# A neighbourhood-attention stage written out over its 28 strips, with another order of work on the engines

## The chip, the cores and the metric

The kernel runs on one core of a Trainium2 chip. The metric is the device time of one execution in microseconds (us), the median of three runs. TensorE (PE in the profile, PEld for its weight loads), VectorE (DVE), ScalarE (ACT), GpSimd (POOL) and SyncE (SP, which here only issues transfers) run side by side and are ordered by semaphores.

## The reference, cut to what matters

Eight images of 128 channels and 56x56 positions go through one block each: group norm, 7x7 neighbourhood attention with 16 heads of 8 channels, a projection and a residual; then full attention over the 3136 positions with 8 heads; then a small dequantised FFN. The part that is changed is the neighbourhood attention:

```python
for a in range(7):
    ka = take(k, si + a, axis=2)                 # si, sj: window start, clipped at the border
    for c in range(7):
        kac = take(ka, sj + c, axis=3)
        logits.append(einsum('bhijd,bhijd->bhij', q, kac) + bias)
attn = softmax(stack(logits, -1), axis=-1)
# out = sum over a, c of attn[..., t] * v at the same neighbour; then out @ proj_w.T + proj_b
```

## The kernel before, in words

All five engines run one loop over the eight images (`b`). Inside an image the stages follow each other: group norm and the q, k, v projections; the neighbourhood stage; projection, layer norm and more projections; the full attention in 14 units (7 blocks of 448 positions, 2 groups of 4 heads); the FFN. The full attention and the other stages are written out; they are not changed.

The neighbourhood stage takes the image in 28 strips of two rows. A strip has 14 units of 2x4 queries, each with a window of 8x10 = 80 keys. All 16 heads and 8 queries of a unit fill the 128 partitions. For strip n:

- POOL `spread_queries` (L467, two instructions): scaled queries times a head mask into `QB`, one of two buffers.
- ACT `keys` (L840): copies the 8 key rows of the window into `KS`, one of two buffers.
- PE `scores` (L602): 112 small float32 matmuls into PSUM banks 0 to 2. These banks exist once, so it waits for the bias additions of the strip before.
- DVE `add_bias` (L1024, five instructions, then L1029): scores plus bias table into the score buffer `SC`, and the negated maximum of each unit.
- POOL `subtract_max` (L472), ACT `exponentials` (L845), DVE `sum_up` (L1033 and L1035: sum and reciprocal), POOL `normalise` (L477): the softmax, in place in `SC`.
- PE `turn` (L613): 14 transposes of `SC` into banks 3, 4, 5, 7; ACT `read_turned` (L853, four instructions) copies them to `PT`.
- PE `values` (L623): 112 small matmuls of the value window `VP` with `PT` into bank 6.
- DVE `finish` (L1040, then L1049 twice): keeps each head's own part and adds it up into `On`.
- SP `load_values` (L374): eight transfers of 70 KB that bring the value window of a strip from DRAM into one of two `VP` buffers, once `values` of the strip two before is done.

`SC` has two buffers, by the strip's parity. Each engine has its order written out by hand, two strips to a pass of an inner loop (`Fori`), with a few strips ahead of and behind the loop outside it. Per strip the orders are:

```
PE    scores(s), turn(s-1), values(s-2)
DVE   add_bias(s), finish(s-2), sum_up(s)
POOL  subtract_max(s), spread_queries(s+2), normalise(s)
ACT   read_turned(s-1), exponentials(s), keys(s+2)
```

An engine takes its instructions in this order, so an instruction that waits holds up all that stand behind it.

Of the kernel before, what the change touches and what calls it, by code (L numbers as in the profile page):

```python
# [15 lines left out]
P = 128  # L16
SIDE = 56
# [112 lines left out]
def hybrid_block(nc, images, x, consts, qkv_wT, rpb, proj_wT, proj_b, Wq, bq, Wk, bk, Wv, bv, Wo, bo,  # L130
# [3 lines left out]
    with ExitStack() as ctx:  # L134
# [54 lines left out]
        KS = part(11088, 2 * WI * WIDE).rearrange("p (s n) -> p s n", s=2)  # L189
        SC = part(15936, 2 * UNITS * KEYS).rearrange("p (s u k) -> p s u k", s=2, u=UNITS)  # L190
# [32 lines left out]
        keys_strip, queries_strip = sem("keys_strip"), sem("queries_strip")  # L223
# [84 lines left out]
        def _(sp):  # L308
# [67 lines left out]
            with sp.Fori(0, images) as b:  # L376
# [10 lines left out]
                load_values(window_row(0), 0)  # L387
                load_values(window_row(1), 1)
                with sp.Fori(1, STRIPS // 2 - 1) as t:
                    for k in range(2):  # L390

                        sp.wait_ge(pv_in, b * STRIPS + (t * 2 + (k - 1 + PRIMED)))
                        apart(sp)
                        load_values(t * 4 + (2 * k - 3), k)
                for k in range(2):
                    s = STRIPS - 2 + k
                    sp.wait_ge(pv_in, b * STRIPS + (s - 1 + PRIMED))
                    load_values(window_row(s), k)
# [44 lines left out]
        def _(pool):  # L443
# [5 lines left out]
            with pool.Fori(0, images) as b:  # L449
# [10 lines left out]
                def spread_queries(tok0, k):  # L460
                    for i in range(QI):
                        src = Qn[:, bass.ds(tok0 + i * SIDE, SIDE)] if not isinstance(tok0, int) else \
                            Qn[:, tok0 + i * SIDE:tok0 + (i + 1) * SIDE]
                        dst = QB[:, k, :, :].rearrange("p u (h i j) -> p u h i j", h=GH, i=QI)[:, :, :, i, :]
                        src = src.rearrange("p (u o j) -> p u o j", o=1, j=QJ).to_broadcast([P, UNITS, GH, QJ])
# [3 lines left out]
                def subtract_max(n, k):  # L469
                    pool.wait_ge(biased, (n + 1) * 6 + PRIMED)  # L470
                    m = NM[:, k, 0:UNITS].rearrange("p (u o) -> p u o", o=1).to_broadcast([P, UNITS, KEYS])
                    nc.gpsimd.tensor_tensor(SC[:, k, :, :], SC[:, k, :, :], m, ALU.add).then_inc(shifted, 1)  # L472

                def normalise(n, k):
                    pool.wait_ge(summed, n * 2 + 2)
                    r = SUMS[:, 1, k, 0:UNITS].rearrange("p (u o) -> p u o", o=1).to_broadcast([P, UNITS, KEYS])
                    nc.gpsimd.tensor_tensor(SC[:, k, :, :], SC[:, k, :, :], r, ALU.mult).then_inc(normalised, 1)  # L477

                wait_freed(pool, b, NQ, NBLK - 1)
                apart(pool)  # L480
                base = b * STRIPS

                def queries(s, k):
                    if not (isinstance(s, int) and s < 2):
                        pool.wait_ge(scores_in, base + (s - 1))
                    spread_queries(s * (QI * SIDE), k)


                queries(0, 0)
                queries(1, 1)  # L490
                with pool.Fori(0, STRIPS // 2 - 1) as t:
                    for k in range(2):
# [3 lines left out]
                for k in range(2):  # L496
                    subtract_max(base + (STRIPS - 2 + k), k)
                    normalise(base + (STRIPS - 2 + k), k)
# [57 lines left out]
        def _(pe):  # L556
# [8 lines left out]
            with pe.Fori(0, images) as b:  # L565
# [26 lines left out]
                def scores(n, k):  # L592
                    pe.wait_ge(keys_strip, n + 1)
                    pe.wait_ge(queries_strip, n * 2 + 2)
                    pe.wait_ge(biased, n * 6 + (PRIMED - 1))
                    apart(pe)
                    win = KS[:, k, :].rearrange("p (y x) -> p y x", x=WIDE)
                    for u in range(UNITS):
                        bk_, at = s_at[u]
                        for g in range(4):  # L600
                            r = slice(32 * g, 32 * g + 32)
                            m = mm(PS[r, bk_, at * KEYS:(at + 1) * KEYS], QB[r, k, u, :],  # L602
                                   win[r, :, u * QJ:u * QJ + WJ], start=True, stop=True,
                                   tile_position=(32 * g, 32 * g))
                    m.then_inc(scores_in, 1)

                def turn(n, k):

                    pe.wait_ge(normalised, n + 1)
                    for c in range(4):  # L610
                        pe.wait_ge(turned_read, n * 4 + (c - 3 + PRIMED))
                        for u in range(4 * c, min(4 * c + 4, UNITS)):
                            m = nc.tensor.transpose(PS[0:KEYS, TURN_BANKS[c], (u % 4) * P:(u % 4 + 1) * P],  # L613
                                                    SC[:, k, u, :], ident)
                        m.then_inc(turned, 1)

                def values(n, k, visit):
                    pe.wait_ge(turned_read, n * 4 + (4 + PRIMED))
                    pe.wait_ge(out_strip, n * 3 + PRIMED)
                    pe.wait_ge(values_in[k], visit)  # L620
# [7 lines left out]
                VIS = 16 * WI  # L628
                per = STRIPS // 2 * VIS

                scores(base, 0)
                scores(base + 1, 1)
                turn(base, 0)
                with pe.Fori(1, STRIPS // 2) as t:
                    scores(base + t * 2, 0)
                    turn(base + (t * 2 - 1), 1)
                    values(base + (t * 2 - 2), 0, b * per + t * VIS)
                    scores(base + (t * 2 + 1), 1)
                    turn(base + t * 2, 0)
                    values(base + (t * 2 - 1), 1, b * per + t * VIS)  # L640
                values(base + (STRIPS - 2), 0, b * per + per)
                turn(base + (STRIPS - 1), 1)
                values(base + (STRIPS - 1), 1, b * per + per)
                pe.wait_ge(out_strip, b * (3 * STRIPS) + 3 * STRIPS + PRIMED)
# [168 lines left out]
        def _(act):  # L813
            nc.scalar.preload_act_table_set("natural_log_exp_and_others")
            act.wait_ge(weights_in, 16 * 22)
            with act.Fori(0, images) as b:
# [15 lines left out]
                wait_freed(act, b, NK, NBLK - 1)  # L832
                act.wait_ge(pads_zero, b * 3 + 3)

                def keys(n, row, k, first):
                    if not first:
                        act.wait_ge(scores_in, n - 1)
                    src = Kn[:, bass.ds(row * WIDE, WI * WIDE)] if not isinstance(row, int) else \
                        Kn[:, row * WIDE:(row + WI) * WIDE]
                    nc.scalar.activation(KS[:, k, :], src, ACT.Copy).then_inc(keys_strip, 1)  # L840

                def exponentials(n, k):
                    act.wait_ge(shifted, n + 1)
                    v = SC[:, k, :, :].rearrange("p u k -> p (u k)")
                    nc.scalar.activation(v, v, ACT.Exp).then_inc(exps, 1)  # L845

                def read_turned(n, k):
                    for c in range(4):
                        act.wait_ge(turned, n * 4 + (c + 1))
                        if c == 0:  # L850
                            act.wait_ge(pv_in, n + (PRIMED - 1))
                        u0, u1 = 4 * c, min(4 * c + 4, UNITS)
                        nc.scalar.activation(PT[0:KEYS, k, u0:u1, :].rearrange("p u e -> p (u e)"),  # L853
                                             PS[0:KEYS, TURN_BANKS[c], 0:(u1 - u0) * P], ACT.Copy).then_inc(turned_read, 1)


                keys(base, window_row(0), 0, True)
                keys(base + 1, window_row(1), 1, True)
                exponentials(base, 0)
                keys(base + 2, window_row(2), 0, False)  # L860
                with act.Fori(1, STRIPS // 2 - 2) as t:
                    read_turned(base + (t * 2 - 2), 0)
                    exponentials(base + (t * 2 - 1), 1)
                    keys(base + (t * 2 + 1), t * 4 - 1, 1, False)
                    read_turned(base + (t * 2 - 1), 1)
                    exponentials(base + t * 2, 0)
                    keys(base + (t * 2 + 2), t * 4 + 1, 0, False)
                for s in range(STRIPS - 5, STRIPS):
                    read_turned(base + (s - 1), (s - 1) % 2)
                    exponentials(base + s, s % 2)  # L870
                    if s + 2 < STRIPS:
                        keys(base + (s + 2), window_row(s + 2), s % 2, False)
                read_turned(base + (STRIPS - 1), 1)
# [76 lines left out]
        def _(dve):  # L950
# [29 lines left out]
            with dve.Fori(0, images) as b:  # L980
# [34 lines left out]
                def add_bias(n, k, row_type, first):  # L1015

                    dve.wait_ge(scores_in, n + 1)
                    if not first:
                        dve.wait_ge(turned, (n - 1) * 4)
# [163 lines left out]
```

## Time and profile before

| what | us |
|---|---|
| median of 3 runs (10486.08 to 10497.13) | 10486.84 |
| time of the profiled execution | 10482.69 |
| its span | 10480.6 |
| PE busy, DVE busy, ACT busy, POOL busy | 8999.7, 8033.9, 6604.5, 1650.4 |

The mean granted TensorE clock is 0.916 of full speed. The digits of the profile's 40 slices repeat every five slices, once for an image: POOL and the data transfers are busy in the first and part of the second slice of each, which is the neighbourhood stage, and PE and DVE read 9 and 7 in the full attention behind it. A busy share of an engine is a mean over such stages, so the stage has to be read by itself.

### The profile page before, as it was taken

What the parts mean: (1) busy time and instruction counts of PE and PEld (TensorE: products, weight loads), DVE (VectorE), ACT (ScalarE), POOL (GpSimd) and SP (SyncE); (2) the same over time, 40 slices, a digit from 0 to 9 for tenths busy, and PEclk for the clock granted to TensorE, in tenths of its full rate; (3) what the DMA queues carried; (4) which work ended last, traced back from release to release, by engine and by line L of the source; (5) the groups of instructions that cost most, each with busy time, mean ns of one, the idle gap of its engine ahead of it and who ended that gap; (6) DMA issues with size and microseconds to landing.
All of it is one profiled execution on the core that took longest, in us unless ns stands there. A gap on an engine that the chain in (4) does not pass through costs nothing.

```text
span 10480.6 us, 426471 instructions
## 1 busy us (share of the span) xinstructions
PE 8999.7 (86%) x166082; PEld 4883.0 (47%) x166082; DVE 8033.9 (77%) x13861; ACT 6604.5 (63%) x13585; POOL 1650.4 (16%) x1701
## 2 busy tenths in 40 slices
PE   5699967999679996799967999679996799967999
PEld 4344453444544545444453444534445344453444
DVE  5699757997579975799757996579965799657996
ACT  3388833888338883388833888338883388734887
POOL 5200042000410004100041000410004100051000
PEclk8799987999879998799987999879998799987999
DMA  3400034000330003300033000430004300033000
GB/s 62 63 3 3 3 57 62 3 3 3 59 60 3 3 3 60 59 3 3 3 61 58 3 3 3 62 57 3 3 3 63 56 3 3 6 60 55 3 3 9
DMA packets 386155, 269.61 MB, mean 26 GB/s; under 512 B 49836, under 2 KB 377244, under 8 KB 383516
## 3 DMA queue, kind: packets, MB, share of 16 engines
q1 hardware_dynamic: 378524, 229.58, 14.0%
q0 software_dynamic: 6144, 19.28, 1.2%
q8 instruction: 1046, 17.14, 0.7%
q14 instruction: 441, 3.61, 0.1%
HBM read 144.03 MB, written 25.86 MB: 16 GB/s over the span
## 4 chain that ended last, share of the span: by engine, by line
PE 65%; issue 20%; POOL 5%; DVE 3%; SPq 3%; ACT 2%; POOLq 1%; DMA 1%; ACTq 0%; DVEq 0%
PE PS L684 21%; PE PS L747 19%; PE PS L725 19%; POOL arena L477 2%; POOL arena L467 2%; SPq L408 2%; DVE block_max L1144 2%; ACT arena L937 1%; PE PS L653 1%; PE PS L715 1%; PE PS L711 1%; PE PS L657 1%; PE PS L574 1%; PE PS L648 1%; SPq L416 0%
## 5 line engine op out<-in xcount | busy, mean ns | idle before, releaser
L1112 DVE TENSOR_REDUCE block_max<-PS 128x1 f32<-128x448 f32 x10192 | 5687.8, 617 | 494.2 <-PE PS L684 361.4
L937 ACT ACTIVATE arena<-PS 128x448 f32<-128x448 f32 (+1 forms) x11200 | 5262.6, 560 | 1161.2 <-PE PS L747 1134.2
L684 PE MATMUL PS<-KP,arena 96*32 96x448 bf16 x43904 | 4142.4, 373 | 354.5 <-DMA KP<-arena 281.0
L747 PE MATMUL PS<-arena,KP 99*32 99x448 bf16 x43904 | 4033.8, 354 | 108.3 <-ACT arena L937 73.6
L725 PE MATMUL PS<-arena 128*32 128x448 f32 x22400 | 2648.9, 540 | 19.3 <-ACT arena L937 14.8
L684 PEld LDWEIGHTS PS<-KP,arena 96*32 96x32 bf16 x43904 | 1294.7, 98 | 2024.4 <-issue 531.7
L747 PEld LDWEIGHTS PS<-arena,KP 99*32 99x32 bf16 x43904 | 1275.9, 96 | 1632.1 <-ACT arena L937 884.1
L853 ACT ACTIVATE arena<-PS 80x512 f32<-80x512 f32 (+1 forms) x896 | 442.9, 537 | 1315.1 <-PE PS L613 1312.1
L613 PE MATMUL PS<-C,arena 128*80 128x128 f32 x3136 | 582.4, 361 | 675.1 <-POOL arena L477 675.1
L526 POOL CAST shift_parts<-shift 14x128 bf16<-14x128 f32 x112 | 31.3, 279 | 5427.7 <-ACT shift L903 5427.7
L725 PEld LDWEIGHTS PS<-arena 128*32 128x32 f32 x22400 | 714.0, 110 | 360.4 <-ACT arena L937 90.6
L613 PEld LDWEIGHTS PS<-C,arena 128*80 128x80 f32 x3136 | 456.9, 155 | 751.8 <-issue 716.6
L1040 DVE TENSOR_TENSOR arena<-PS,C 128x448 f32<-128x448 f32 x224 | 139.6, 623 | 705.9 <-PE PS L623 705.8
L602 PE MATMUL PS<-arena 32*32 32x80 f32 x25088 | 528.7, 235 | 109.3 <-issue 47.9
L477 POOL TENSOR_TENSOR arena<-arena 128x1120 f32<-128x1120 f32 x224 | 461.7, 2061 | 757.3 <-DVE arena L1035 757.3
L602 PEld LDWEIGHTS PS<-arena 32*32 32x32 f32 x25088 | 484.8, 108 | 138.9 <-issue 133.2
L1144 DVE TENSOR_REDUCE block_max<-PS 128x2 f32<-128x896 f32 x336 | 388.3, 1234 | 170.4 <-PE PS L684 170.4
L472 POOL TENSOR_TENSOR arena<-arena 128x1120 f32<-128x1120 f32 x224 | 461.3, 2060 | 355.8 <-DVE arena L1029 355.8
L903 ACT ACTIVATE shift<-PS 14x128 f32<-14x128 f32 x112 | 28.0, 250 | 686.3 <-PE PS L705 686.3
L1024 DVE TENSOR_TENSOR arena<-PS,nat_bias 128x80 f32<-128x80 f32 (+3 forms) x1120 | 353.9, 382 | 119.9 <-PE PS L602 88.5
L1127 DVE TENSOR_TENSOR X<-X,PS 128x448 f32<-128x448 f32 x56 | 34.8, 621 | 481.8 <-PE PS L715 481.8
L539 POOL TENSOR_TENSOR normed<-tail 128x448 f32<-128x448 f32 x112 | 127.9, 1142 | 1623.0 <-ACT tail L919 1623.0
(98 smaller groups left out, 4893.7 us busy)
## 6 DMA issues: line engine op xcount, KB each, us to landing
arena<-vT_padded SPq DMA_DIRECT2D x1792, 70.0 KB
arena<-arena SPq DMA_DIRECT2D x384, 98.0 KB, 4.3
KP<-arena POOLq DMA_DIRECT2D x192, 98.0 KB, 8.9
KP<-arena SPq DMA_DIRECT2D x192, 98.0 KB, 4.7
arena<-in_x SPq DMA_DIRECT2D x9, 1568.0 KB, 6.7
vT_padded<-arena SPq DMA_DIRECT2D x16, 784.0 KB
out_y<-X SPq DMA_DIRECT2D x56, 224.0 KB, 2.5
arena<-shift_parts SPq DMA_DIRECT2D x336, 3.5 KB
```

The source lines that it names most:

```text
L472: nc.gpsimd.tensor_tensor(SC[:, k, :, :], SC[:, k, :, :], m, ALU.add).then_inc(shifted, 1)
L477: nc.gpsimd.tensor_tensor(SC[:, k, :, :], SC[:, k, :, :], r, ALU.mult).then_inc(normalised, 1)
L602: m = mm(PS[r, bk_, at * KEYS:(at + 1) * KEYS], QB[r, k, u, :], win[r, :, u * QJ:u * QJ + WJ], start=True, stop=True, tile_position=(32 * ...
L613: m = nc.tensor.transpose(PS[0:KEYS, TURN_BANKS[c], (u % 4) * P:(u % 4 + 1) * P], SC[:, k, u, :], ident)
L684: ins = mm(PS[at:at + QT, bank, 0:BLK], QP[0:ROWS, g, unit_queries(unit, h, t, QT)], KP[0:ROWS, g, h, j * BLK:(j + 1) * BLK], start=True, ...
L725: m = mm(PS[32 * h:32 * h + 32, 6, 0:BLK], VA[:, c, unit[0] * GH + h, :], exp_buffer(c)[:, h, :], start=(c == 0), stop=(c == CHUNKS - 1), ...
L747: ins = mm(PS[k0:k0 + 32, at % banks, 0:BLK], KP[0:ROWSM, g, h, c * P + k0:c * P + k0 + 32], QP[0:ROWSM, g, unit_queries(unit, h)], start= ...
L853: nc.scalar.activation(PT[0:KEYS, k, u0:u1, :].rearrange("p u e -> p (u e)"), PS[0:KEYS, TURN_BANKS[c], 0:(u1 - u0) * P], ACT.Copy).then_i ...
L937: nc.scalar.activation(exp_buffer(c)[0:n, h, :], PS[0:n, bank, 0:BLK], ACT.Exp, scale=float(ADIM) ** -0.5).then_inc(exp_done, 1)
L1024: V.tensor_tensor(SC[:, k, u0:u1, :], PS[:, bk_, at:at + m * KEYS].rearrange("p (u k) -> p u k", u=m), nat_bias[:, row_type, kind:kind + 1 ...
L1112: V.tensor_reduce(block_max[:, q, j:j + 1], PS[:, max_banks()[0][m][0], 0:BLK], AX.X, ALU.max).then_inc(max_read, 1)
L1144: V.tensor_reduce(block_max[:, m // NBLK, j0:j1], PS[:, j0:j1, 0:BLK], AX.X, ALU.max).then_inc(max_read, j1 - j0)
```

## The change

The inner loops of the neighbourhood stage go, on all five engines; the 28 strips are written out with fixed addresses. `SC` gets four buffers, taken by the strip's number modulo four. `keys` and its buffer `KS` go: `scores` reads the padded key image `Kn` itself. The second and third instruction of `finish` become one. The orders per step s become:

```
PE    turn(s-2), scores(s+1), values(s-2)
DVE   add_bias(s), sum_up(s-1), finish(s-3)
POOL  subtract_max(s), normalise(s-1), spread_queries(s+2)
ACT   read_turned(s-2), exponentials(s)
```

The core of the diff:

```diff
-        SC = part(15936, 2 * UNITS * KEYS).rearrange("p (s u k) -> p s u k", s=2, u=UNITS)
+        SC = [part(at, UNITS * KEYS).rearrange("p (u k) -> p u k", u=UNITS) for at in (15936, 17056, 28608, 29728)]
+        NSC = len(SC)
@@ SyncE
-                load_values(window_row(0), 0)
-                load_values(window_row(1), 1)
-                with sp.Fori(1, STRIPS // 2 - 1) as t:
...
+                for s in range(STRIPS):
+                    if s >= 2:
+                        sp.wait_ge(pv_in, b * STRIPS + (s - 1 + PRIMED))
+                    load_values(window_row(s), s % 2)
@@ GpSimd
-                with pool.Fori(0, STRIPS // 2 - 1) as t:
-                    for k in range(2):
-                        subtract_max(base + (t * 2 + k), k)
-                        queries(t * 2 + (k + 2), k)
-                        normalise(base + (t * 2 + k), k)
...
+                for s in range(STRIPS + 1):
+                    if s < STRIPS:
+                        subtract_max(s)
+                    if s >= 1:
+                        normalise(s - 1)
+                    if s + 2 < STRIPS:
+                        spread_queries(s + 2)
@@ TensorE
-                    win = KS[:, k, :].rearrange("p (y x) -> p y x", x=WIDE)
-                                   win[r, :, u * QJ:u * QJ + WJ], start=True, stop=True,
+                                   k_img[r, row:row + WI, u * QJ:u * QJ + WJ], start=True, stop=True,
-                with pe.Fori(1, STRIPS // 2) as t:
-                    scores(base + t * 2, 0)
-                    turn(base + (t * 2 - 1), 1)
-                    values(base + (t * 2 - 2), 0, b * per + t * VIS)
...
+                wait_freed(pe, b, NK, NBLK - 1)
+                scores(0)
+                for s in range(STRIPS + 2):
+                    if s >= 2:
+                        turn(s - 2)
+                    if s + 1 < STRIPS:
+                        scores(s + 1)
+                    if s >= 2:
+                        values(s - 2)
@@ ScalarE
-                def keys(n, row, k, first):
...
+                for s in range(STRIPS + 2):
+                    if s >= 2:
+                        read_turned(s - 2)
+                    if s < STRIPS:
+                        exponentials(s)
@@ VectorE
-                    if not first:
-                        dve.wait_ge(turned, (n - 1) * 4)
+                    if s >= NSC:
+                        dve.wait_ge(turned, (base + (s - NSC + 1)) * 4)
-                    for i in range(QI):
...
-                        V.tensor_reduce(o.rearrange("p (u j) -> p u j", u=UNITS), v[:, i], AX.X,
-                                        ALU.add).then_inc(out_strip, 1)
+                    o = On[:, s * ROW:(s + 1) * ROW].rearrange("p (i u j) -> p i u j", i=QI, u=UNITS)
+                    V.tensor_reduce(o, v, AX.X, ALU.add).then_inc(out_strip, 1)
-                with dve.Fori(1, STRIPS // 2 - 1) as t:
-                    for k in range(2):
-                        add_bias(base + (t * 2 + k), k, 2, False)
-                        finish(base + (t * 2 + (k - 2)), k, t * (2 * ROW) + (k - 2) * ROW)
-                        sum_up(base + (t * 2 + k), k)
...
+                for s in range(STRIPS + 3):
+                    if s < STRIPS:
+                        add_bias(s)
+                    if 1 <= s <= STRIPS:
+                        sum_up(s - 1)
+                    if s >= 3:
+                        finish(s - 3)
```

`values(s)` waits for `finish(s-1)` and for its loads, `spread_queries(s)` for `scores(s-2)`, `scores(s)` for the bias additions of strip s-1, each `read_turned(s)` for `values(s-2)`, as before.

## Rows read from the trace of the kernel before

**Rows 1.** The page's first line: span and number of instructions.

```profile
span 10480.6 us, 426471 instructions
```

**Rows 2.** Windows: stretch, length, busy us of PE, PEld, DVE, ACT, POOL; clock, DMA share, GB/s.

```profile
70.10:350.40 280.30, 178.62 (x6665) 155.89 (x6665) 169.19 (x308) 98.47 (x167) 142.27 (x108) 0.83 0.44 63
...
500.00:1300.00 800.00, 788.56 (x12933) 381.19 (x12929) 702.36 (x1266) 651.01 (x1393) 33.00 (x65) 1.00 0.01 3
```

**Rows 3.** Waits from 100 to 320 us: total us, times, longest us.

```profile
DVE arena L1040 <- PE PS L623: 72.3, 23, 3.7
```

**Rows 4.** Timeline of one strip: start us, us, instruction, [idle before it, what ended it].

```profile
191.76 0.62 DVE L1040 TENSOR_TENSOR arena<-PS,C 128x448 f32<-128x448 f32 x1 [3.36 <-PE PS L623]
...
192.55 1.04 DVE L1049 TENSOR_REDUCE arena<-arena 128x224 f32 x2 [0.17 <-DVE arena L1040]
193.51 1.31 DVE L1033 TENSOR_REDUCE arena<-arena 128x14 f32<-128x1120 f32 x1
194.85 0.24 DVE L1035 RECIPROCAL arena<-arena 128x14 f32<-128x14 f32 x1
195.13 1.58 DVE L1024 TENSOR_TENSOR arena<-PS,nat_bias 128x80 f32<-128x80 f32 x5
195.18 2.06 POOL L477 TENSOR_TENSOR arena<-arena 128x1120 f32<-128x1120 f32 x1 [3.60 <-DVE arena L1035]
196.75 1.32 DVE L1029 TENSOR_REDUCE arena<-arena 128x14 f32<-128x1120 f32 x1
...
197.37 3.18 PE L613 MATMUL PS<-C,arena 128*80 128x128 f32 x14 [3.30 <-POOL arena L477]
...
200.48 1.30 PE L623 MATMUL PS<-arena 96*32 96x32 f32 x112
...
201.81 0.62 DVE L1040 TENSOR_TENSOR arena<-PS,C 128x448 f32<-128x448 f32 x1 [3.74 <-PE PS L623]
```

**Rows 5.** Groups by shape from 100 to 320 us: busy us, mean ns of one.

```profile
L472 POOL TENSOR_TENSOR arena<-arena 128x1120 f32<-128x1120 f32 x23 | 47.4, 2060 | 25.1 <-DVE arena L1029 25.1
L853 ACT ACTIVATE arena<-PS 80x512 f32<-80x512 f32 x69 | 39.2, 591 | 137.4 <-PE PS L613 137.1
...
L845 ACT ACTIVATE arena<-arena 128x1120 f32<-128x1120 f32 x23 | 26.1, 1134 | 4.2 <-POOL arena L472 4.2
L467 POOL TENSOR_TENSOR arena<-arena,C 128x224 f32<-128x224 f32 x46 | 24.7, 558 | 0.0
```

**Rows 6.** Timeline of PE, another strip.

```profile
178.96 1.72 PE L613 MATMUL PS<-C,arena 128*80 128x128 f32 x14 [3.40 <-POOL arena L477]
180.62 1.16 PE L623 MATMUL PS<-arena 96*32 96x32 f32 x112
```

**Rows 7.** Windows inside the stage, to read the granted clock.

```profile
177.00:180.40 3.40, 1.44 (x13) 1.45 (x14) 2.63 (x5) 0.69 (x2) 2.49 (x2) 1.00 0.71 84
187.50:190.50 3.00, 3.00 (x14) 2.38 (x14) 0.90 (x1) 1.47 (x3) 2.02 (x2) 0.50 0.27 29
```

**Rows 8.** Timeline of PE, second image, the first two strips' scores.

```profile
1376.83 2.15 PE L602 MATMUL PS<-arena 32*32 32x80 f32 x112 [1.47 <-ACT arena L840]
...
1383.95 0.35 PE L602 MATMUL PS<-arena 32*32 32x80 f32 x4 [2.86 <-issue]
```

**Rows 9.** Transfers by queue from 500 to 1300 us: packets, MB, share of 16 engines.

```profile
q8 instruction: 112, 1.84, 1.0%
```

**Rows 10.** The same from 100 to 330 us.

```profile
q8 instruction: 1, 0.02, 0.0%
```

**Rows 11.** The same from 1381.7 to 1382.8 us.

```profile
q8 instruction: 1, 0.02, 5.5%
```

**Rows 12.** The same from 1385.2 to 1386.3 us.

```profile
q8 instruction: 1, 0.02, 5.4%
```

**Rows 13.** Window in which two strips' value loads run back to back.

```profile
1387.00:1397.00 10.00, 5.96 (x147) 4.92 (x139) 5.67 (x12) 3.69 (x6) 6.39 (x5) 0.74 0.74 116
```

More of the change, by code:

```diff
@@ L457, in _, with spread_queries @@
                 apart(pool)
-                def spread_queries(tok0, k):
+                base = b * STRIPS
+                def spread_queries(s):
+                    if s >= 2:
+                        pool.wait_ge(scores_in, base + (s - 1))
                     for i in range(QI):
[L462 to L465, printed above, removed]
+                        tok0 = (s * QI + i) * SIDE
+                        dst = QB[:, s % 2, :, :].rearrange("p u (h i j) -> p u h i j", h=GH, i=QI)[:, :, :, i, :]
+                        src = Qn[:, tok0:tok0 + SIDE].rearrange("p (u o j) -> p u o j", o=1, j=QJ) \
+                            .to_broadcast([P, UNITS, GH, QJ])
@@ L474, in normalise, with subtract_max @@
[L474 to L477, printed above, removed]
+                def subtract_max(s):
+                    pool.wait_ge(biased, (base + (s + 1)) * 6 + PRIMED)
+                    m = NM[:, s % 2, 0:UNITS].rearrange("p (u o) -> p u o", o=1).to_broadcast([P, UNITS, KEYS])
+                    nc.gpsimd.tensor_tensor(SC[s % NSC], SC[s % NSC], m, ALU.add).then_inc(shifted, 1)
@@ L479, in _, with normalise @@
+                def normalise(s):
+                    pool.wait_ge(summed, base * 2 + (s * 2 + 2))
+                    r = SUMS[:, 1, s % 2, 0:UNITS].rearrange("p (u o) -> p u o", o=1).to_broadcast([P, UNITS, KEYS])
+                    nc.gpsimd.tensor_tensor(SC[s % NSC], SC[s % NSC], r, ALU.mult).then_inc(normalised, 1)
                 wait_freed(pool, b, NQ, NBLK - 1)
                 apart(pool)
[L481 to L486, printed above, removed]
@@ L489, in _ @@
-                queries(0, 0)
-                queries(1, 1)
-                with pool.Fori(0, STRIPS // 2 - 1) as t:
-                    for k in range(2):
-                        subtract_max(base + (t * 2 + k), k)
-                        queries(t * 2 + (k + 2), k)
-                        normalise(base + (t * 2 + k), k)
-                for k in range(2):
-                    subtract_max(base + (STRIPS - 2 + k), k)
-                    normalise(base + (STRIPS - 2 + k), k)
+                spread_queries(0)
@@ L590, in _, with scores @@
                 s_at = [(0, u) if u < 5 else (1, u - 5) if u < 10 else (2, u - 10) for u in range(UNITS)]
[L592 to L595, printed above, removed]
+                k_img = Kn.rearrange("p (y x) -> p y x", x=WIDE)
+                def scores(s):
+                    row = window_row(s)
+                    pe.wait_ge(queries_strip, base * 2 + (s * 2 + 2))
+                    pe.wait_ge(biased, (base + s) * 6 + (PRIMED - 1))
                     apart(pe)
-                    win = KS[:, k, :].rearrange("p (y x) -> p y x", x=WIDE)
                     for u in range(UNITS):
@@ L626, in values @@
                     m.then_inc(pv_in, 1)
[L628 to L633, printed above, removed]
-                with pe.Fori(1, STRIPS // 2) as t:
-                    scores(base + t * 2, 0)
-                    turn(base + (t * 2 - 1), 1)
-                    values(base + (t * 2 - 2), 0, b * per + t * VIS)
[L638 to L644, printed above, removed]
+                wait_freed(pe, b, NK, NBLK - 1)
[7 more added lines that the diff above has]
+                        values(s - 2)
+                pe.wait_ge(out_strip, b * (2 * STRIPS) + 2 * STRIPS + PRIMED)
                 for j in range(NBLK):
@@ L831, in _ @@
                 base = b * STRIPS
-                wait_freed(act, b, NK, NBLK - 1)
                 act.wait_ge(pads_zero, b * 3 + 3)
-                def keys(n, row, k, first):
-                    if not first:
[L837 to L840, printed above, removed]
@@ L842, in exponentials, with read_turned @@
-                def exponentials(n, k):
-                    act.wait_ge(shifted, n + 1)
-                    v = SC[:, k, :, :].rearrange("p u k -> p (u k)")
+                def exponentials(s):
+                    act.wait_ge(shifted, base + (s + 1))
+                    v = SC[s % NSC].rearrange("p u k -> p (u k)")
                     nc.scalar.activation(v, v, ACT.Exp).then_inc(exps, 1)
-                def read_turned(n, k):
+                def read_turned(s):
                     for c in range(4):
-                        act.wait_ge(turned, n * 4 + (c + 1))
+                        act.wait_ge(turned, (base + s) * 4 + (c + 1))
@@ L850, in read_turned @@
                         if c == 0:
-                            act.wait_ge(pv_in, n + (PRIMED - 1))
+                            act.wait_ge(pv_in, base + (s + PRIMED - 1))
                         u0, u1 = 4 * c, min(4 * c + 4, UNITS)
-                        nc.scalar.activation(PT[0:KEYS, k, u0:u1, :].rearrange("p u e -> p (u e)"),
+                        nc.scalar.activation(PT[0:KEYS, s % 2, u0:u1, :].rearrange("p u e -> p (u e)"),
                                              PS[0:KEYS, TURN_BANKS[c], 0:(u1 - u0) * P], ACT.Copy).then_inc(turned_read, 1)
-                keys(base, window_row(0), 0, True)
@@ L858, in _ @@
[L858 to L873, printed above, removed]
+                for s in range(STRIPS + 2):
+                    if s >= 2:
+                        read_turned(s - 2)
+                    if s < STRIPS:
+                        exponentials(s)
@@ L1013, in _, with add_bias @@
                 dve.wait_ge(vpad_out, 32)
-                def add_bias(n, k, row_type, first):
-                    dve.wait_ge(scores_in, n + 1)
-                    if not first:
-                        dve.wait_ge(turned, (n - 1) * 4)
+                def add_bias(s):
+                    row_type = s if s < 2 else 2 if s < STRIPS - 2 else s - (STRIPS - 5)
+                    dve.wait_ge(scores_in, base + (s + 1))
+                    if s >= NSC:
+                        dve.wait_ge(turned, (base + (s - NSC + 1)) * 4)
                     for bk_, u0, u1, kind in ((0, 0, 1, 0), (0, 1, 5, 1), (1, 5, 10, 1), (2, 10, 13, 1), (2, 13, 14, 2)):
@@ L1024, in add_bias, with sum_up, finish @@
                         V.tensor_tensor(
-                            SC[:, k, u0:u1, :], PS[:, bk_, at:at + m * KEYS].rearrange("p (u k) -> p u k", u=m),
+                            SC[s % NSC][:, u0:u1, :], PS[:, bk_, at:at + m * KEYS].rearrange("p (u k) -> p u k", u=m),
                             nat_bias[:, row_type, kind:kind + 1, :].to_broadcast([P, m, KEYS]),
                             ALU.add).then_inc(biased, 1)
-                    dve.wait_ge(biased, n * 6 + 5 + PRIMED)
-                    V.tensor_reduce(NM[:, k, 0:UNITS], SC[:, k, :, :], AX.X, ALU.max, negate=True).then_inc(biased, 1)
-                def sum_up(n, k):
-                    dve.wait_ge(exps, n + 1)
-                    V.tensor_reduce(SUMS[:, 0, k, 0:UNITS], SC[:, k, :, :], AX.X, ALU.add).then_inc(summed, 1)
-                    dve.wait_ge(summed, n * 2 + 1)
-                    V.reciprocal(SUMS[:, 1, k, 0:UNITS], SUMS[:, 0, k, 0:UNITS]).then_inc(summed, 1)
-                def finish(n, k, tok0):
-                    dve.wait_ge(pv_in, n + (1 + PRIMED))
+                    dve.wait_ge(biased, (base + s) * 6 + (5 + PRIMED))
+                    V.tensor_reduce(NM[:, s % 2, 0:UNITS], SC[s % NSC], AX.X, ALU.max, negate=True).then_inc(biased, 1)
+                def sum_up(s):
+                    dve.wait_ge(exps, base + (s + 1))
+                    V.tensor_reduce(SUMS[:, 0, s % 2, 0:UNITS], SC[s % NSC], AX.X, ALU.add).then_inc(summed, 1)
+                    dve.wait_ge(summed, (base + s) * 2 + 1)
+                    V.reciprocal(SUMS[:, 1, s % 2, 0:UNITS], SUMS[:, 0, s % 2, 0:UNITS]).then_inc(summed, 1)
+                def finish(s):
+                    dve.wait_ge(pv_in, base + (s + 1 + PRIMED))
                     V.tensor_tensor(PVM.rearrange("p (u h q) -> p u h q", u=UNITS, h=GH),
```

48 lines of the change are left out of this document (13 added, 35 removed).

## The prediction

> **What bounds the kernel now.** I read the page's first line [rows 1], then windows by stage, then in the stage that changes the waits, the timeline of one strip, and the groups by shape. The neighbourhood stage of the first image runs from its first scores at 70.1 to the projection at 350.4 us: 280.3 us, with PE busy 64%, DVE 60%, POOL 51% and ACT 35% [rows 2]. No engine is the bound there; a chain is. For eight images it is 8 x 280.3 = 2242 us of the 10480.6. The full attention behind it has PE busy 98.6% at full clock [rows 2] and isn't touched.
>
> DVE's largest wait is the one for `values`, 3.1 us a strip [rows 3]. The timeline shows why: DVE has `finish` ahead of `sum_up`, so the strip's chain closes on itself. `finish` at 191.76, its sums 192.55, sum 193.51, reciprocal 194.85, POOL's `normalise` 195.18 (2.06), the transposes 197.37 (3.18), `values` 200.48 (1.30), and `finish` again at 201.81 [rows 4]: 10.05 us, all serial. The mean period follows from the stage. One strip alone passes scores 2.15 [rows 8], additions and maximum 2.9 [rows 4], subtract 2.06, exponential 1.13 [rows 5], sum and reciprocal 1.55, normalise 2.06 [rows 4], transposes about 2.5 (1.72 to 3.18) [rows 4, 6], the last eviction 0.4 to 0.6 [rows 5], values 1.2 [rows 6], finish 1.4 to 1.7 [rows 4]: some 17.5 us. Then 280.3 = 27 periods + 17.5, a period of 9.73 us.
>
> **The change part by part.** The new orders put `sum_up(s-1)` in front of `finish(s-3)`, so no engine waits for a strip that is just under way. I price each engine's strip, since the longest of them now sets the period.
>
> DVE: additions 1.58, maximum 1.32, sum 1.31, reciprocal 0.24, mask 0.62 [rows 4]. The two sums of `finish`, 0.52 each for 224 elements, become one of 448. The rows give (1.31 - 0.52) / (1120 - 224) = 0.88 ns an element, so 0.52 + 0.20 = 0.72; the bounds are 0.52 (no dearer than one) and 1.04 (no gain). With some 0.28 of small handovers: **6.07 us** (5.9 to 6.4).
>
> POOL: 2 x 2.06 + 2 x 0.56 [rows 4, 5] = 5.24, with handovers 5.5. The duration of POOL's 2.06 us instruction is the same beside DVE's additions and beside an idle DVE, so I add nothing for the greater overlap. ACT: four evictions of at most 0.59 and an exponential of 1.13 [rows 5], 3.5; the removed `keys` was never on the path. That `scores` reads `Kn` with the row step that `KS` had too I price at nothing, bounds -0.1 to +0.3 us a strip on PE.
>
> PE: transposes 1.72, values 1.16 [rows 6], scores 2.15 [rows 8], three gaps of 0.2: **5.63 us** at full clock. The transposes took 1.72 at 2.4 GHz and 3.2 at 1.2 GHz, the lower level coming after PE had stood idle some 2.7 us [rows 4, 6, 7]. With PE working over 80% of a period such gaps go, and I take the full clock. If the lower stayed in each strip's transposes PE would need 7.1.
>
> Value loads: two strips' loads run back to back at 116 GB/s [rows 13]; 8 x 70 KB at that rate are 4.9 us a strip, under any period above. From `values(s-2)` to `values(s)` there are now about 11 us, against the some 7 of a lone load: 4.9 at that rate and 2 for issue and landing. Hidden; and since two periods only have to hold 7 + 1.2, the loads would set no period above 4.9 even if they came last.
>
> The crossed chains, by the new orders: subtract, normalise, transposes, scores, additions, maximum closes after two strips: 2.06 + 2.06 + 1.72 + 2.15 + 1.58 + 1.32 and about 0.7 of handovers = 11.6, 5.8 a strip. Finish, values, transposes, scores, additions, maximum, sum: 1.4 + 1.16 + 1.72 + 2.15 + 2.9 + 1.55 and 0.6 = 11.5, 5.7 a strip. Both lie under DVE's 6.07. DVE's wait for a free `SC` is for a strip four back: never late. SP's waits hold only its own loads.
>
> **What the unrolling brings.** The inner loop's code is fetched once: one instruction packet of 16 KB in 230 us [rows 10]. Written-out code is fetched as it runs: 112 packets in 800 us of full attention for 12933 + 12929 PE instructions, 231 and some waits each, one in 7.1 us [rows 2, 9]. A strip has (14 + 112 + 112) x 2 = 476 PE instructions, about 1.95 packets, so one in 3.1 us at DVE's period. What a packet that isn't there costs is seen once: in the second image PE stops inside the second strip's scores for 2.86 us with nothing to wait for; the packet runs in that stop, between 1381.7 and 1382.8 [rows 8, 11]. Execution resumes at 1383.95 and the next packet starts only after 1385.2 [rows 12], one block ahead of what runs. Counted from there it would be usable some 1.25 + (1383.95 - 1381.7) = 3.5 us after the block before began. So I take 2.9 to 3.5, say 3.3 us, as the least time between two blocks. `values` and part of `scores`, 256 instructions, pass in 1.16 + 0.2 + 0.3 = 1.7 us, or in 2.0 where the border falls in its middle: PE then stands 1.3 to 1.6 us. The block with the transposes takes about 3.7 and doesn't wait. With 1.1 to 1.4 us lost in most strips, PE's strip goes from 5.63 to 6.8 (6.3 at 2.9, 7.1 at 3.5). Bounds from the rows: nothing, as in the full attention, and two stops of 2.86 a strip, 11.4.
>
> A rule of the Trainium skill bears on this (Runtime: NRT & Kernel Launch, Instruction fetch mechanics): the sequencer fetches the next block while the current one runs, which hides it because instructions issue slower than blocks arrive, and kernels prefer full unrolling to branches. The full attention agrees, at one block in 7.1 us; the stop of 2.86 us does not. By the rule the sum would be DVE's case below, by the row the one that I take.
>
> **The sum.** Period 6.8: 27 x 6.8 + 17.5 = 201.1 us, 79.2 less than 280.3, for eight images 634. 10482.7 - 634 = 9849 for the profiled execution; the median lies 4 above it, so about **9853 us**. The one-time starts of a stage (the first loads, the first stop for code) are in both and cancel.
>
> **The rivals.**
> 1. *DVE sets the period.* Blocks arrive in time: 6.07 a strip, 27 x 6.07 + 17.5 = 181.4, 98.9 less, 791 in all: 9696 us. For it: no stop for code in the full attention, and in the first pass of the inner loop, where PE's code is new too, turn, values and scores ran without a gap. Against: only PE's two fast groups ask for blocks this fast.
> 2. *Code and clock together.* Fetches slow down beside the value loads (DMA share 0.44 now [rows 2], some 0.63 at 6.8), or PE's stops bring the lower clock back so that the transposes take 3.2 again. A period near 8: 233.5, 46.8 less, 374 in all, 10112 us. For it: both levels alternate in this stage now [rows 7]. Against: stops of 1.5 us are shorter than the idle stretches that precede the low level.
> 3. *Slower than before.* Each block is asked for too late under load. PE goes from one block to the next in L us, 1.95 a strip; it decides from L = 9.73 / 1.95 = 5.0. With two full stops a strip of 2.86 the period is 5.63 + 5.72 = 11.4: 325 us a stage, 45 more, 360 in all, 10847 us. For it: such a stop exists [rows 8]. Against: it comes once in the code of two strips, beside the writes of the padded values, and the rest of that code runs through.
>
> **How the numbers follow.** Forecast, period 6.4 to 7.4: 0.46. DVE's case: 0.34. The third case, 7.4 to 9.6: 0.14. Slower, 0.04; within 0.2%, which is about what a measurement of this kernel can tell from no change: 0.02. Faster therefore 0.94. The range takes in DVE's case down to 9680 (a period of 6.0) and the forecast's to a period of 7.55, 10016: 9680 to 10020. Inside the likeliest case alone it is 9767 to 9983.
>
> **What would show it.** In the profile after: the stage at about 201 us (181 for DVE's case); DVE's wait for `values` gone; q8 packets in the stage some 55 an image and no closer than 3.3 us; PE idle before `scores` or in its middle put down to issue, about 1.1 us a strip; the clock 1.00 throughout; L1049 half as often, at about 0.72. DVE without gaps would prove me wrong towards 9700. Wrong altogether would be a period over 9.7, or transposes still at 3.2.

## The result, and the profile after

The changed kernel takes 10150.9 us (median of 4 runs, 10123.3 to 10186.7) against 10486.5 before: ratio 0.9681, interval 0.9649 to 0.9713. That is 336 us less, where 634 were forecast, and outside the stated range of 9680 to 10020. The profiled execution is the fastest of its runs, 10123.3 us, 359 under the one before.

The page of the changed kernel and its windows (stretch, length, busy us of PE, PEld, DVE, ACT, POOL, clock, DMA share, GB/s), to set beside [rows 1, 2]:

```profile
span 10121.2 us, 420263 instructions
...
69.10:300.23 231.13, 167.36 (x6664) 147.26 (x6664) 164.12 (x280) 83.74 (x140) 141.27 (x108) 0.88 0.54 81
```

The first image's stage went from 280.3 to 231.1 us. From first scores to projection the stages of the eight images were 2231.5 us in all and are 1873.6 now, 234.2 each: 357.9 of the 359.4 us come from there; all the rest of the execution moved by 1.5 us. With the 17.5 us of one strip's passage the period, the time from one strip to the next, is (234.2 - 17.5) / 27 = 8.03 us, not 6.8.

The waits of the changed kernel from 100 to 290 us (total us, times, longest us), about 24 strips:

```profile
ACT arena L827 <- PE PS L601: 116.2, 39, 7.6
POOL arena L468 <- DVE arena L991: 69.1, 24, 5.7
DVE arena L986 <- PE PS L590: 45.0, 21, 4.5
PEld PS L612 <- issue: 44.5, 23, 4.2
PE PS L612 <- issue: 40.6, 21, 4.1
```

DVE's wait for `values` [rows 3] is gone; DVE waits for `scores` (L590) instead. ACT waits for the transposes, POOL for DVE, DVE for PE, and PE, before or inside `values` (L612), for nothing that the profile shows: 40.6 us, 1.7 a strip. The timeline of PE and its neighbours in one strip, beside [rows 4]:

```profile
165.94 2.15 PE L590 MATMUL PS<-arena 32*32 32x80 f32 x112
...
168.01 0.53 PE L612 MATMUL PS<-arena 96*32 96x32 f32 x37
168.24 1.58 DVE L986 TENSOR_TENSOR arena<-PS,nat_bias 128x80 f32<-128x80 f32 x5 [3.23 <-PE PS L590]
...
171.71 0.85 PE L612 MATMUL PS<-arena 96*32 96x32 f32 x75 [3.17 <-issue]
```

`values` is one run of 112 matmuls without a wait between them. PE does 37, stands still for 3.17 us and does the other 75. No semaphore stands there; a block of code does not. The queues of the same stage, from 69.1 to 300.23 us, then from 100 to 290 us (packets, MB, share of 16 engines):

```profile
q8 instruction: 54, 0.88, 1.7%
```

```profile
q8 instruction: 46, 0.75, 1.8%
```

Before it was one packet in 230 us [rows 10]. Now it is 46 in 190 us, one in 4.13.

That mean alone shows no cause: a strip holds 1.95 blocks, so a period of 8.03 us gives it whatever sets the period. The stops tell more. I take the inner part of each stage, from 30 us after the first scores to 10 us before the projection, in all eight images. There PE stood still for more than 0.7 us inside a group of matmuls 182 times. From the start of the last packet to the matmul that resumes the median is 2.66 us, from there to the start of the next packet 1.41, and from packet to packet 4.11. The shortest distance between two packets of the stage is 3.28 us.

### The profile page after: what moved, and what is told of

The parts are those of the page before. It is cut to its first block, busy times and chain, and to the rows that moved or that the text cites. A ratio compares the mean times of both kernels' runs of the same rounds, so it can differ in the third digit from the quotient of the medians.

```text
span 10121.2 us, 420263 instructions
## 1 busy us (share of the span) xinstructions
PE 8905.5 (88%) x166082; PEld 4676.6 (46%) x166082; DVE 7995.4 (79%) x13637; ACT 6473.8 (64%) x13361; POOL 1653.8 (16%) x1701
## 4 chain that ended last, share of the span: by engine, by line
PE 78%; issue 11%; DVE 3%; SPq 3%; ACT 2%; DMA 1%; POOL 1%; ACTq 0%; DVEq 0%; POOLq 0%
PE PS L666 21%; PE PS L729 20%; PE PS L707 20%; PE PS L590 4%; PE PS L601 4%; PE PS L612 3%; SPq L400 2%; DVE block_max L1094 2%; ACT arena L898 1%; PE PS L635 1%; PE PS L697 1%; PE PS L693 1%; PE PS L639 1%; PE PS L561 1%; PE PS L630 1%
## 5 line engine op out<-in xcount | busy, mean ns | idle before, releaser
L666 PEld LDWEIGHTS PS<-KP,arena 96*32 96x32 bf16 x43904 | 1233.3, 98 | 2084.9 <-issue 544.9
L729 PEld LDWEIGHTS PS<-arena,KP 99*32 99x32 bf16 x43904 | 1227.4, 96 | 1684.4 <-ACT arena L898 905.6
L707 PEld LDWEIGHTS PS<-arena 128*32 128x32 f32 x22400 | 681.4, 110 | 385.7 <-ACT arena L898 90.6
L612 PE MATMUL PS<-arena 96*32 96x32 f32 x25088 | 310.1, 203 | 388.5 <-issue 351.4
L590 PE MATMUL PS<-arena 32*32 32x80 f32 x25088 | 569.0, 242 | 94.0 <-issue 52.9
L590 PEld LDWEIGHTS PS<-arena 32*32 32x32 f32 x25088 | 507.1, 113 | 168.0 <-issue 167.5
L601 PE MATMUL PS<-C,arena 128*80 128x128 f32 x3136 | 495.5, 321 | 51.0 <-issue 33.4
L612 PEld LDWEIGHTS PS<-arena 96*32 96x32 f32 x25088 | 266.8, 114 | 439.6 <-issue 402.6
L601 PEld LDWEIGHTS PS<-C,arena 128*80 128x80 f32 x3136 | 399.4, 139 | 87.5 <-issue 58.2
```

Of the source, the lines that this page charges most:

```text
L590: m = mm(PS[r, bk_, at * KEYS:(at + 1) * KEYS], QB[r, s % 2, u, :], k_img[r, row:row + WI, u * QJ:u * QJ + WJ], start=True, stop=True, til ...
L612: m = mm(PS[32 * g:32 * g + 32, 6, 32 * u:32 * u + 32], VP[0:KPAD, k, u, 32 * g:32 * g + 32], PT[0:KPAD, k, u, 32 * g:32 * g + 32], start= ...
L666: ins = mm(PS[at:at + QT, bank, 0:BLK], QP[0:ROWS, g, unit_queries(unit, h, t, QT)], KP[0:ROWS, g, h, j * BLK:(j + 1) * BLK], start=True, ...
L707: m = mm(PS[32 * h:32 * h + 32, 6, 0:BLK], VA[:, c, unit[0] * GH + h, :], exp_buffer(c)[:, h, :], start=(c == 0), stop=(c == CHUNKS - 1), ...
L729: ins = mm(PS[k0:k0 + 32, at % banks, 0:BLK], KP[0:ROWSM, g, h, c * P + k0:c * P + k0 + 32], QP[0:ROWSM, g, unit_queries(unit, h)], start= ...
```

## The experiments

Stage lengths are means over the eight images of the profiled execution, from first scores to projection.

**TensorE in a loop again.** All engines keep the new orders and stay written out, but TensorE loops over two strips. For static addresses the key rows are copied as before and the normalised scores go to one of two buffers.

```diff
+        SC = [...three buffers...]; SN = [...two buffers...]     # normalise: SC[s % 3] -> SN[s % 2]
-                for s in range(STRIPS + 2):
-                    if s >= 2:
-                        turn(s - 2)
...
+                with pe.Fori(1, STRIPS // 2 - 1) as t:
+                    turn(base + (t * 2 - 2), 0)
+                    scores(base + (t * 2 + 1), 1)
+                    values(base + (t * 2 - 2), 0, b * per + t * VIS)
+                    turn(base + (t * 2 - 1), 1)
+                    scores(base + (t * 2 + 2), 0)
+                    values(base + (t * 2 - 1), 1, b * per + t * VIS)
```

> The new orders on every engine, but TensorE keeps a loop of two strips (static addresses: the key rows are copied as in the kernel before, and the normalised scores go to one of two buffers of their own, with three score buffers before them). The other engines stay written out. Theory (TensorE's period of 8.0 us in the changed kernel is set by fetching its written-out code, one block in about 4.1 us, 1.95 blocks a strip): fetches in the stage fall from 54 an image to 10 to 14, the stops inside the matmul groups go, the transposes stay at full clock, and VectorE sets the period at 6.1 to 6.5 us: a stage of 182 to 195 us instead of 234, some 9710 to 9810 us in all. Rival (the stops are a data wait that the order itself makes, for the evictions or for bank 6): the period stays at 7.9 to 8.1, 10120 to 10180 us.

Measured: 9760.2 us (9732.7 to 9771.3), ratio to before 0.930, interval 0.928 to 0.932, the fastest version that computes everything. Stage 190.0 us, a period of 6.39. The instruction packets of its first stage, the stage's window, and one strip of DVE:

```profile
q8 instruction: 12, 0.20, 0.4%
```

```profile
69.20:263.79 194.59, 153.58 (x6664) 137.07 (x6664) 161.91 (x280) 97.29 (x167) 141.16 (x108) 0.90 0.67 92
```

```profile
171.31 0.57 DVE L1024 TENSOR_TENSOR arena<-PS,C 128x448 f32<-128x448 f32 x1
171.91 0.99 DVE L1031 TENSOR_REDUCE arena<-arena 128x112 f32<-128x448 f32 x1
...
172.82 1.57 DVE L1008 TENSOR_TENSOR arena<-PS,nat_bias 128x80 f32<-128x80 f32 x5
...
174.42 1.32 DVE L1013 TENSOR_REDUCE arena<-arena 128x14 f32<-128x1120 f32 x1
175.66 1.31 DVE L1017 TENSOR_REDUCE arena<-arena 128x14 f32<-128x1120 f32 x1
...
177.00 0.24 DVE L1019 RECIPROCAL arena<-arena 128x14 f32<-128x14 f32 x1
177.16 0.56 DVE L1024 TENSOR_TENSOR arena<-PS,C 128x448 f32<-128x448 f32 x1
```

Twelve blocks instead of 54, and DVE goes through this strip without a gap in 5.85 us, 171.31 to 177.16. In the middle of the loop the strips take about 5.6 and 6.2 us in turn, so this is nearly the first rival of the prediction, brought about. One expectation held only in part: the transposes of 32 of the 224 strips still take over 2.6 us, against 89 in the changed kernel.

**Its control: the same kernel, TensorE written out.** One line differs, so the copied keys and the buffers are the same.

```diff
-                with pe.Fori(1, STRIPS // 2 - 1) as t:
+                for t in range(1, STRIPS // 2 - 1):
```

> The control for the kernel with TensorE's loop of two strips: the same buffers, copied key rows and orders, the same instructions, but TensorE's 24 middle strips written out. Theory (code): 54 blocks an image again, period 7.9 to 8.2, 10110 to 10200 us. Rival (the copied key rows or the separate buffers for the normalised scores made the gain): it stays at 9740 to 9790 us.

Measured: 10138.2 us (10116.9 to 10147.6), ratio to before 0.966, interval 0.964 to 0.968; 54 blocks an image, stage 237.1 us. The 378 us between this and the kernel above are the price of written-out code on TensorE, with what follows from it: 83 strips, not 32, have transposes of over 2.6 us.

**Half of the values matmuls left out.**

```diff
-                    for u in range(UNITS):
+                    for u in range(0, UNITS, 2):     # in values
```

> The changed kernel with every second unit of the values matmuls left out (56 of 112 a strip, so their part of the output is not computed). Theory (code): 364 and some 14 instructions a strip instead of 490, 1.5 blocks at 4.1 us: a period of 6.2 to 6.6, a stage of 185 to 196 us, 9740 to 9830 us. Rival (data waits or the matmuls' own time): the group is 0.6 us shorter and the period 7.4 to 8.0, 9990 to 10120 us.

Measured: 9835.6 us, one run; stage 195.6 us, 6.60 a strip: 6 us above what the code theory gave, 154 under its rival. 42 blocks in the first stage's 197.0 us. A strip lost 1.4 us, while the removed matmuls take 0.6.

**One value load of eight.** The others' values are stale.

```diff
-                    load_values(window_row(s), s % 2)
+                    load_values(window_row(s), s % 2, WI if s < 2 else 1)
```

> The changed kernel with one of the eight value loads a strip from the third strip on (the others' values are stale). Theory, with contention (the value loads, at 0.56 of the transfer engines' time, slow the fetches from 3.3 to 4.1 us a block): blocks come every 3.2 to 3.5 us, the period falls to 6.4 to 7.0, 9790 to 9920 us. Theory without contention (4.1 us is what a fetch takes anyway): spacing and period stay, 10100 to 10180 us. Rival (the value loads themselves are late and hold up values): the period falls to 6.1 with the block spacing then following it, about 9700 us.

Measured: 9964.4 us, one run; stage 216.0 us, 7.35 a strip. The window of its first stage and its code packets from 100 to 275 us:

```profile
69.70:285.89 216.19, 157.45 (x6664) 138.40 (x6664) 163.87 (x280) 82.41 (x140) 141.16 (x108) 0.94 0.12 26
```

```profile
q8 instruction: 44, 0.72, 1.8%
```

The time fell between two of the forecasts. With a DMA share of 0.12 instead of 0.54 a block comes every 3.98 us in this stretch, where it was 4.13. Over the inner part of all eight images the mean distance of packets is 3.92 against 4.25, and at the stops the median is 3.88 against 4.11. So a block comes 0.2 to 0.3 us sooner without the loads, and most of its time isn't contention.

The period fell by 0.68 us. Of TensorE's time a strip, idle time put down to issue fell from 1.95 to 1.56 us and busy time, with the clock at 0.94 instead of 0.88 in the first stage, from 5.96 to 5.74. The rest is TensorE's waits for late value loads, which in the whole execution of the changed kernel were these (us, times, longest), 0.08 us a strip:

```profile
PE PS L612 <- DMA arena<-vT_padded: 18.9, 11, 3.4
```

**The same on the loop version.** The edit is the one above, on the kernel with TensorE's loop.

> The kernel with TensorE's loop of two strips, and one of the eight value loads a strip from the third strip on (the others' values are stale). That kernel's stage took 190 us on average, 6.39 a strip, while VectorE's uninterrupted strip in it is 5.85 us. Theory (some value loads come late: TensorE waited 71 us in all for them before values): the period falls to 5.9 to 6.0 and the stage to 177 to 180, 80 to 100 us less in all, 9660 to 9690 us. Rival (the first written-out strips and single stops for code make the difference): 9730 to 9770 us.

Measured: 9711.6 us, one run; stage 183.9 us, 6.16 a strip. Between the two forecasts: of the 0.54 us a strip between 6.39 and DVE's 5.85, late value loads make 0.23. The rest lies at the ends of the stage: in the middle of the loop the strips now take 5.6 and 6.1 us in turn, 5.85 on average, while the first two take 7.8 and 8.0.

**A loop body of four strips.** Four score buffers, normalised in place.

```diff
-                with pe.Fori(1, STRIPS // 2 - 1) as t:
...
+                with pe.Fori(0, 6) as t:
+                    for j in range(4):
+                        turn(base + (t * 4 + j), j)
+                        scores(base + (t * 4 + (j + 3)), (j + 1) % 2)
+                        values(base + (t * 4 + j), j % 2, b * per + t * (2 * VIS) + (j // 2 + 1) * VIS)
```

> The same with a loop body of four strips on TensorE, some 1960 instructions or 7.8 blocks, with four score buffers normalised in place. Theory A (TensorE keeps fewer blocks than the body has): each pass fetches anew, some 54 blocks an image as in the written-out kernel, period 7.9 to 8.1 or worse by a stop at each jump back, 10120 to 10250 us. Theory B (the body fits): 15 to 18 blocks an image and a stage of 185 to 200 us, 9720 to 9830 us.

Measured: 10332.8 us (10317.6 to 10374.2), ratio to before 0.987, interval 0.984 to 0.989; stage 260.0 us. The first stage's packets:

```profile
q8 instruction: 66, 1.08, 2.0%
```

66 blocks, more than written out. A body of 3.9 blocks is kept from pass to pass, one of 7.8 isn't. Each jump back then adds a stop: from one strip's transposes to the next it is 13.4 us on average across a jump and 8.0 elsewhere. So this is the worst of both, beyond the upper end that I gave. Its score buffers differ from those of the two-strip loop as well; the 8.0 us away from the jumps, as in the written-out kernels, speak against them as the cause.

**The orders of before, all written out.** Two score buffers, copied keys, the merged sum kept.

```diff
-                    if 1 <= s <= STRIPS:
-                        sum_up(s - 1)
-                    if s >= 3:
-                        finish(s - 3)
+                    if s >= 2:
+                        finish(s - 2)
+                    sum_up(s)                        # and the other engines' orders of before
```

> The orders of the kernel before, two score buffers and the copied key rows, but all strips written out on all engines (one merged sum in finish kept). Theory (code): the serial chain of 9.7 us a strip leaves TensorE idle for 3 us, during which a block can arrive, but the stops inside values and scores lie on that chain: 1 to 3 us a strip more, 10.4 to 12 a strip, 10650 to 11050 us. If the stops hide in the chain's idle time: 9.3 to 9.7 a strip, 10380 to 10490 us.

Measured: 10428.9 us, one run; stage 274.3 us, 9.51 a strip. My first theory missed and the second one held. TensorE waits for the chain anyway, 3.0 us a strip for `normalise` in the kernel before and 2.1 here, and much of the fetching hides there: idle time put down to issue is 1.0 us a strip, where the changed kernel has 1.95. Written-out code costs what it delays.

**Two score buffers.** The rest is the changed kernel.

```diff
-        SC = [...] for at in (15936, 17056, 28608, 29728)]
+        SC = [...] for at in (15936, 17056)]
```

> The changed kernel with two score buffers instead of four, all strips written out. The additions of strip s then wait for the transposes of strip s-2, which wait for its normalisation. Theory (the buffers are what lets the chain open): subtract, normalise, transposes, additions and maximum close on themselves, 2.06 + 2.06 + 1.72 to 3.2 + 2.9 and handovers, 9.4 to 10.2 a strip, a stage of 270 to 292 us: 10420 to 10600 us. Rival (the order alone is enough and buffers are not used): 10120 to 10190 us.

Measured: 10631.3 us, one run; stage 298.1 us, 10.4 a strip, slower than the kernel before. DVE's additions now wait for the transposes (100 to 240 us):

```profile
DVE arena L986 <- PE PS L601: 64.0, 13, 8.4
```

The buffers are needed, and the size is a little beyond what I gave. What makes the excess isn't shown. Idle time of TensorE put down to issue is only 0.36 us a strip here; its scores, which my sum had left out, take 3.74 us at 161.37, against 2.15 in the changed kernel at 165.94.

**Three score buffers.**

```diff
-        SC = [...] for at in (15936, 17056, 28608, 29728)]
+        SC = [...] for at in (15936, 17056, 28608)]
```

> The changed kernel with three score buffers instead of four. Theory (additions of strip s wait for the transposes of strip s-3, which in the new order lie a step back): nothing is late, 10110 to 10190 us. Rival (the stops for code make a fourth buffer necessary): the period grows by 0.3 to 1 us, 10200 to 10400 us.

Measured: 10174.0 us, one run, inside the changed kernel's own spread (10123 to 10187). The fourth buffer brings nothing that this one run can tell.

**The swap alone.** The kernel before with VectorE's `sum_up(s)` ahead of `finish(s-2)`.

```diff
-                        finish(base + (t * 2 + (k - 2)), k, t * (2 * ROW) + (k - 2) * ROW)
                         sum_up(base + (t * 2 + k), k)
+                        finish(base + (t * 2 + (k - 2)), k, t * (2 * ROW) + (k - 2) * ROW)
```

> The kernel before with one edit: VectorE does sum_up(s) ahead of finish(s-2). Theory (what opens the chain is that the softmax steps work on different strips, not the swap): VectorE now waits for the exponential of its own strip, additions and maximum 2.9, subtract 2.1, exponential 1.2, sum 1.55, finish 1.7 and handovers, 9.6 a strip and up: 10430 to 10700 us. Rival (finish ahead of sum_up was the whole fault): a period under 8.5, 10200 us or less.

Measured: 10475.8 us, one run; stage 277.5 us, 9.63 a strip. That is 3 us below the fastest run of the kernel before, nothing that one run can tell. DVE now waits for the exponentials instead of `values` (50.1 us in 15 strips, 100 to 240 us): one closed chain was exchanged for another of the same length. The gain needs the sum a strip behind, and so a third buffer.

## Why the prediction was wrong

The direction, the place, the open chain and written-out code on TensorE as the new limit were right; one term of the sum was too small, and the full clock was taken for granted. One small error lies in the base: the first image's 280.3 us stood for all eight, whose mean is 278.9, 11 us in the sum.

- *A chain of one strip bounds the stage.* Right. It opened: DVE's wait for `values` went [rows 3]. With two buffers, where another chain closes through the score buffer, a strip takes 10.4 us.
- *DVE 6.07 a strip.* The loop version shows 5.85. Inside it the merged sum takes 0.99 us, not 0.72. I had scaled by elements from a sum of 80 neighbours to sums of four; 0.99 is hardly under the two of before, 1.04 together [rows 4]. The merge is worth next to nothing. The handovers cost nothing either: the strip's instructions add up to 6.01 us and overlap a little.
- *PE 5.63, POOL 5.5, ACT 3.5, nobody in DVE's way.* Nearly right for the loop version: DVE waits for `scores` 55 times in eight images, 190 us in all. The value loads I called hidden come late in some strips: 0.23 us a strip there.
- *1.95 blocks a strip, 54 or 55 an image, fetched one ahead.* Right: 54, and leaving out the loop on TensorE alone costs 378 us.
- *"So I take 2.9 to 3.5, say 3.3 us, as the least time between two blocks."* **This is the step that failed.** As the least time it is right: the shortest distance in the stage is 3.28 us. But the sum used it as the time that every block takes, and at the stops blocks come 4.11 us apart. I had one reading: 2.25 us from the packet's start to the matmul that resumes, and 1.25 from there to the next packet [rows 8, 11, 12]. The medians at 182 stops are 2.66 and 1.41, and idle time put down to issue is 1.95 us a strip. The same working with 4.1 gives: the block with `values` passes in 1.7 to 2.0 us, so PE stands 2.1 to 2.4 us, and 5.63 + 2.1 to 2.4 is 7.7 to 8.0 a strip; measured 8.03. Without the value loads it is 3.88 us, so they are the smaller part of the difference. The trace of before had a second reading: in the first image's scores PE stops for 2.90 us and resumes at 77.27, and the queues of that stretch, 74.9 to 79.2 us (packets, MB, share), show two packets, which begin at 74.97 and 79.04, 4.07 us apart:

```profile
q8 instruction: 2, 0.03, 2.7%
```

- *The clock.* I took full clock throughout. A stop of 2.60 and one of 3.17 us, as at 161.83 and 171.71, do what the idle stretches of before did [rows 7]: the transposes behind the first, at 162.92, take 3.09 us, and their window shows the lower of the two levels. It is the smaller part. From one strip's transposes to the next, in the inner strips of the eight images, it takes 7.73 us on average where the transposes take under 1.9 us (101 strips) and 8.57 where they take over 2.6 (71); the mean of all 184 is 8.07. So the lower clock makes some 0.3 us of the 1.23 that I missed.

```profile
162.90:166.00 3.10, 3.10 (x24) 2.55 (x22) 2.04 (x4) 1.45 (x3) 3.10 (x2) 0.54 0.24 67
```

What happened is the second rival, code and clock together, at 8.0 a strip: it had 0.14. Its time of 10112 us lies near the measured 10151, in part by luck, since its "near 8" was not worked out. Both of its causes are there, and neither is enough. Without nearly all value loads the period falls by 0.68 us, to 7.35; the clock makes some 0.3. But in that run the strips whose transposes run at full clock still take 7.30 us, 0.5 over my 6.8, and of what was named only the pace of the blocks is left for that.

DVE's case, which a rule of the Trainium skill supported (Runtime: NRT & Kernel Launch, Instruction fetch mechanics: the next block comes while the current one runs), isn't seen for this code. The measurements decide: at one block in 7.1 us the fetch is hidden [rows 9], at the pace of these matmul groups it is not, and unrolling, which the Trainium skill says that kernels prefer to branches, lost 378 us on TensorE.

The range was too narrow for the same reason. The bounds of this term, from the rows, ran from nothing to two stops of 2.86 us a strip, a period of 11.4, and I let the range follow a narrow guess inside them.

## What to carry to other kernels

Before writing out a loop, count the engine's instructions per microsecond. TensorE got a block of some 250 instructions (54 blocks for 28 strips of about 490) every 4 us here, so groups of tiny matmuls (112, with as many weight loads, in 1.2 us) outrun it, and a loop of two strips (3.9 blocks) beat the written-out code by 3.7% with everything else equal, while one of four strips lost to both. Keep a loop with static addresses, at the price of a small copy, on the engine with many instructions. The other engines were written out in every version with the new orders, so whether that helps them no run here tells.

When a hand-written order closes a chain on itself, look for the step that can work one strip behind and for the buffer it needs: the swap without the buffer gained nothing, the order with two buffers lost 1.4%, three were enough.

## What the runs showed of the hardware that I had not expected

- A stop for code sits in the middle of a run of matmuls, as idle time put down to issue. Its median is 1.8 us among those of over 0.7. Behind stops of 2.60 and 3.17 us the next group ran at the lower clock (transposes 3.09 instead of 1.73 us).
- At these stops a block takes 4.11 us from packet to packet with the value loads running and 3.88 without nearly all of them; no two packets of the changed kernel's stage begin less than 3.28 us apart.
- TensorE kept a loop body of 3.9 blocks from pass to pass (12 packets an image) and fetched one of 7.8 blocks again each time (66).
- A sum over groups of four on DVE takes 0.99 us for 448 elements, where a sum over groups of 80 takes 1.31 us for 1120.
